# One pass per sorted block of tokens instead of two masked experts: the mixture stage of a one-core transformer kernel

## The chip, the cores and the metric

The kernel runs on 1 core of one Trainium2 chip. The metric is the device time of one execution in microseconds (us). Besides the engines (TensorE for matrix products, VectorE, ScalarE, GpSimd and SyncE, which issues the plain transfers) the core has 16 transfer (DMA) engines. In the profile they are named PE (with PEld for its weight loads), DVE, ACT, POOL and SP.

## The reference, cut to what matters

The input is 4096 tokens (2 x 2048) of 256 floats. Six residual stages follow each other: a mixture stage, a linear attention, the same mixture stage again (same weights), an FP4 feed-forward, a softmax attention, and the FP4 feed-forward again. The change touches the two mixture stages only. Each computes

```
gate_scores = xf @ gate_w.T                       # two experts
one_hot = one_hot(argmax(softmax(gate_scores)))
masked = xf[None] * one_hot.T[:, :, None]         # zero rows for the expert not chosen
h = relu(einsum('end,edh->enh', masked, w1) + b1[:, None, :])
expert_out = einsum('enh,ehd->end', h, w2) + b2[:, None, :]
routing_output = expert_out.sum(axis=0)
shared = relu(xf @ sw1 + sb1) @ sw2 + sb2
x = x + 0.5 * (routing_output + shared)           # xf is the layer-normalised x
```

with 256 features and 1024 hidden units. The expert that is not chosen sees a zero row and so still adds the constant `relu(b1) @ w2 + b2`.

## The kernel before

Everything is written as one program of raw blocks; within a block each engine's instructions stand in the order written, and semaphores order the engines against each other. `x` stays in on-chip memory as 32 tiles of 128 tokens. Products are made at nearly full precision: each operand is split into a rounded part (`hi`) and a remainder (`lo`), and three matmuls (hi x hi, hi x lo, lo x hi) are summed.

The mixture stage, `ffn0(tag)`, is called twice, with tag "a" and tag "b". It works through G = 8 groups of 4 tiles (512 tokens). A group has 24 steps: 8 hidden chunks of 128 units for each of the shared expert and the two routed ones. A step s has these parts:

- TensorE, `up(g, s)` (lines 365 to 376): 6 matmuls of 512 columns into one PSUM bank of three.
- ScalarE, `hidden` (lines 433 to 449): two activations, the rounded and the full relu. For the routed steps VectorE first multiplies by the mask (`masking`, line 525), which zeroes the hidden sums of tokens that belong to the other expert.
- VectorE, `low` (line 531): the remainder, full minus rounded.
- TensorE, `down(g, s - 2)` (lines 378 to 393): 12 matmuls of 256 columns, which add to the group's output banks.

Once in a group TensorE also makes the gate's product (line 409, 6 matmuls of 512 columns), and VectorE two masks of it (lines 516 and 517). The normalised tokens of the next group are made by VectorE (`normal`), transposed by TensorE after steps 18 and 21 (line 349), copied by ScalarE (`evacuate`, line 425) and completed by VectorE (`low_x`, line 503) in steps 19 and 22. The next group's first `up` waits for that, two steps later. `finish` (line 540) adds the group's output to x and makes the statistics for the next stage's layer norm (`tile_stats`, lines 119 and 121).

Weights come in pieces of 128x512 through two buffers (line 333). At the start eight pieces of the shared expert are split, by GpSimd (lines 605 and 607) and by ScalarE and VectorE in turn (lines 453 and 509); then come three bias rows, which in call "a" stand in SP's queue behind seven loads of x (line 336), and VectorE sums them (lines 570 and 574) before its first `low`; then GpSimd splits the 16 pieces of the two routed experts.

Of the kernel before, what the change touches and what calls it, by code (L numbers as in the profile page):

```python
# [9 lines left out]
I32 = mybir.dt.int32  # L10
ALU = mybir.AluOpType
# [3 lines left out]
P = 128  # L15
# [41 lines left out]
def build_program(nc, A):  # L57
# [21 lines left out]
    with ExitStack() as ctx:  # L79
# [153 lines left out]

        def ffn0(tag):
            with ExitStack() as scope:
                w1 = [sb(f"w1{p}_{tag}", [P, NE, KD, H0], F32R, scope) for p in ("hi", "lo")]
                w2 = [sb(f"w2{p}_{tag}", [P, NE, C0, D], F32R, scope) for p in ("hi", "lo")]
                b1 = sb(f"b1_{tag}", [P, NE * C0], scope=scope)
                b2h = sb(f"b2h_{tag}", [P, D], scope=scope)
                gate_w = [sb(f"gate_{p}_{tag}", [P, KD, P], F32R, scope) for p in ("hi", "lo")]  # L240
                gcol = sb(f"gate_cols_{tag}", [P, KD, NE - 1], scope=scope)
                gdiff = sb(f"gate_diff_{tag}", [P, KD], scope=scope)
                XN = ring(scope, f"xn{tag}", [P, D], 2)
                XT = ring_of_pairs(scope, f"xT{tag}", [P, KD, GW], 2)
                mask = sb(f"mask{tag}", [P, NE - 1, GW], scope=scope)
                HB = ring(scope, f"hid{tag}", [P, GW], 2)
                HS = ring_of_pairs(scope, f"hs{tag}", [P, GW], 3)
                RAW = ring(scope, f"raw{tag}", [P, GW], 2)

                raw_in = [event(f"f0_raw_in{i}", 16) for i in range(2)]  # L250
                turned, gcol_ok, gate_ok, b1_ok, b2_ok = (event(f"f0_{n}") for n in ("turned", "gcol", "gate", "b1", "b2"))
                split_hi, split_pool, split_vec = (event(f"f0_split_{n}") for n in ("hi", "pool", "vec"))
                xn_ok, xturn, xhi, xlo = (event(f"f0_{n}") for n in ("xn", "xturn", "xhi", "xlo"))
                stat_in, std_g, prod, gmask = (event(f"f0_{n}") for n in ("stat_in", "std", "prod", "gmask"))
                masked, hid_ok, low_ok, down_ok = (event(f"f0_{n}") for n in ("masked", "hid", "low", "down"))
                biased, done = event("f0_biased"), event("f0_done")

                NP = 2 * C0 // 2
                STEPS = NE * C0
                PPG = STEPS + 1  # L260

                def place(g, s):

                    return g * PPG + s + (1 if s >= 4 else 0)

                def read_of(n):

                    g, i = divmod(n, PPG)
                    if i == 4:
                        return gmask(g + 1)  # L270
                    s = i - (1 if i > 4 else 0)
                    if s < C0:
                        return hid_ok(g * STEPS + s + 1)
                    return masked(g * 2 * C0 + s - C0 + 1)
# [4 lines left out]

                def item_of(ex, p):  # L280
                    return 2 + p if ex == 0 else 13 + (ex - 1) * NP + p

# [7 lines left out]
                def piece_dst(ex, p):  # L290
                    if p < 4:
                        return [w[:, ex, p % 2, p // 2 * GW:(p // 2 + 1) * GW] for w in w1]
                    return [w[:, ex, 2 * (p - 4):2 * (p - 4) + 2, :].rearrange("p c d -> p (c d)") for w in w2]

                def piece_ok(ex, p):

                    if ex == 0:
                        return split_vec(p // 2 + 1) if p % 2 else split_pool(p // 2 + 1)
                    return split_pool(4 + (ex - 1) * NP + p + 1)

                def raw_free(item):
                    if item < 2:
                        return turned(item + 1)
                    if item < 10:
                        return piece_ok(0, item - 2)
                    if item < 13:
                        return b2_ok(item - 9)
                    return piece_ok(1 + (item - 13) // NP, (item - 13) % NP)

                with nc.Block() as block:  # L310

                    @block.sync
                    def _(e):
                        e.dma_start(RAW[0][0:2, 0:D], A["L0_ffn_gate_w"]).then_inc(*raw_in[0].up)
# [25 lines left out]
                    def _(e):  # L340
                        def transposes(g, i):
# [3 lines left out]
                            if n:  # L345
                                e.wait_ge(*xlo(n))
# [1575 lines left out]
```

## Time and profile before

| | us |
|---|---|
| three timed runs | 3766.29, 3769.75, 3779.08; median 3769.75 |
| the profiled execution | 3781.05 |
| its span, first to last instruction | 3779.3 |
| first mixture stage, first product to last | about 19.2 to 606 |
| second mixture stage, first product to last | about 968.5 to 1547.5 |

All durations below come from the one profiled execution. Busy TensorE time is modelled, since its matmuls overlap: the distance between the starts of two neighbouring matmuls says how fast they follow each other, while the duration of one is longer. Start times are us from the span's start.

### The profile page before, as it was taken

What the parts mean: (1) busy time and instruction counts of PE and PEld (TensorE: products, weight loads), DVE (VectorE), ACT (ScalarE), POOL (GpSimd) and SP (SyncE); (2) the same over time, 40 slices, a digit from 0 to 9 for tenths busy, and PEclk for the clock granted to TensorE, in tenths of its full rate; (3) what the DMA queues carried; (4) which work ended last, traced back from release to release, by engine and by line L of the source; (5) the groups of instructions that cost most, each with busy time, mean ns of one, the idle gap of its engine ahead of it and who ended that gap; (6) DMA issues with size and microseconds to landing.
All of it is one profiled execution on the core that took longest, in us unless ns stands there. A gap on an engine that the chain in (4) does not pass through costs nothing. (4 is left out here: it accounts for less than half of the span.)

```text
span 3779.3 us, 57424 instructions
## 1 busy us (share of the span) xinstructions
PE 3535.4 (94%) x22274; PEld 2399.2 (63%) x22274; DVE 2698.2 (71%) x4907; ACT 2136.2 (57%) x3830; POOL 600.5 (16%) x504
## 2 busy tenths in 40 slices
PE   6999998999799999799789999999999999999799
PEld 6888886777688888799534433333333333333798
DVE  4545544786454454799478888889889999882898
ACT  3444443443344444455327777777777777766555
POOL 4000001444400000355200000000000000000565
PEclk9999999999899999899969999899999999888899
DMA  3000001000200000000240211111021120000000
GB/s 116 1 1 1 1 1 40 2 2 1 72 1 1 1 1 1 1 1 1 64 50 13 46 24 21 16 20 17 9 28 14 22 28 8 2 2 1 6 18 23
DMA packets 34455, 63.93 MB, mean 17 GB/s; under 512 B 4309, under 2 KB 23433, under 8 KB 31113
## 3 DMA queue, kind: packets, MB, share of 16 engines
q1 hardware_dynamic: 34184, 60.27, 8.5%
q8 instruction: 177, 2.90, 0.3%
q14 instruction: 94, 0.76, 0.1%
HBM read 47.02 MB, written 13.11 MB: 16 GB/s over the span
## 5 line engine op out<-in xcount | busy, mean ns | idle before, releaser
L1836 DVE TENSOR_REDUCE smxp<-psum 128x1 f32<-128x512 f32 x2048 | 1276.3, 682 | 175.3 <-PE psum L1701 168.8
L1796 ACT ACTIVATE spr<-psum 128x512 f32<-128x512 f32 x2048 | 1082.3, 599 | 470.9 <-PE psum L1720 462.2
L1720 PE MATMUL psum<-sqs,sks 50*128 50x512 f32 x2048 | 754.6, 470 | 6.4 <-ACT spr L1796 3.1
L1701 PE MATMUL psum<-sks,sqs 48*128 48x512 f32 x2048 | 677.1, 457 | 29.5 <-DMA sqs<-q_parts 29.1
L1701 PEld LDWEIGHTS psum<-sks,sqs 48*128 48x128 f32 x2048 | 292.3, 198 | 538.7 <-issue 461.3
L1734 PE MATMUL psum<-spr,sv 128*32 128x512 f32 x4096 | 576.8, 636 | 1.8 <-ACT spr L1796 0.7
L1720 PEld LDWEIGHTS psum<-sqs,sks 50*128 50x128 f32 x2048 | 323.1, 194 | 200.9 <-ACT spr L1796 170.0
L1455 POOL MEMSET fhqb<- 128x64 f32 x3 | 0.3, 152 | 1668.9 <-POOLq L1616 1668.9
L389 PE MATMUL psum<-w2hi_a,hsa_hi 128*128 128x256 f32 x768 | 217.2, 283 | 16.8 <-DVE hsa_lo L531 16.8
L389 PE MATMUL psum<-w2hi_b,hsb_hi 128*128 128x256 f32 x768 | 217.3, 283 | 9.2 <-DVE hsb_lo L531 9.2
L389 PE MATMUL psum<-w2lo_b,hsb_hi 128*128 128x256 f32 x768 | 217.8, 284 | 0.0
L389 PE MATMUL psum<-w2lo_a,hsa_hi 128*128 128x256 f32 x768 | 217.7, 283 | 0.0
L389 PE MATMUL psum<-w2hi_a,hsa_lo 128*128 128x256 f32 x768 | 217.3, 283 | 0.0
L389 PE MATMUL psum<-w2hi_b,hsb_lo 128*128 128x256 f32 x768 | 217.3, 283 | 0.0
L525 DVE TENSOR_TENSOR hidb<-psum,maskb 128x512 f32<-128x512 f32 x128 | 88.3, 690 | 173.3 <-PE psum L355 173.3
L531 DVE TENSOR_TENSOR hsb_lo<-hidb,hsb_hi 128x512 fp32r<-128x512 f32 x192 | 147.3, 768 | 84.1 <-ACT hidb L444 75.8
L531 DVE TENSOR_TENSOR hsa_lo<-hida,hsa_hi 128x512 fp32r<-128x512 f32 x192 | 146.4, 763 | 83.8 <-ACT hida L444 75.4
L525 DVE TENSOR_TENSOR hida<-psum,maska 128x512 f32<-128x512 f32 x128 | 88.1, 688 | 158.9 <-PE psum L355 158.9
L447 ACT ACTIVATE hsb_hi<-hidb,b_b 128x512 fp32r<-128x512 f32 x128 | 92.6, 724 | 183.7 <-DVE hidb L525 183.7
L447 ACT ACTIVATE hsa_hi<-hida,b_a 128x512 fp32r<-128x512 f32 x128 | 92.7, 724 | 173.5 <-DVE hida L525 173.5
L1734 PEld LDWEIGHTS psum<-spr,sv 128*32 128x32 f32 x4096 | 82.9, 110 | 152.9 <-issue 126.5
L389 PEld LDWEIGHTS psum<-w2hi_a,hsa_hi 128*128 128x128 f32 x768 | 146.1, 190 | 28.2 <-DVE hsa_lo L531 20.5
(345 smaller groups left out, 7183.3 us busy)
## 6 DMA issues: line engine op xcount, KB each, us to landing
sks<-q_parts SPq DMA_DIRECT2D x48, 256.0 KB, 8.9
sqs<-q_parts SPq DMA_DIRECT2D x48, 256.0 KB, 20.0
q_parts<-spart SPq DMA_DIRECT2D x16, 512.0 KB, 2.7
x<-in_L_attn_x_dram SPq DMA_DIRECT2D x8, 512.0 KB, 7.3
rawa<-in_L_ffn_w_dram SPq DMA_DIRECT2D x16, 256.0 KB
rawb<-in_L_ffn_w_dram SPq DMA_DIRECT2D x16, 256.0 KB
out_dram<-x SPq DMA_DIRECT2D x8, 512.0 KB, 2.9
rawa<-in_L_ffn_sw_dram SPq DMA_DIRECT2D x8, 256.0 KB
```

What stands on the lines that cost most here:

```text
L389: m = e.matmul(ops[:, i // 2, (i % 2) * D:(i % 2 + 1) * D], hs[u][:, i * P:(i + 1) * P], w2[v][:, ex, c, :], start=(s == 0 and i % 2 == 0 ...
L447: e.activation(hi[:], hid[:], ACT.Relu, bias=bias).then_inc(*sc.up())
L525: e.tensor_tensor(HB[n % 2][:], psum[:, j % 3, :], mask[:, s // C0 - 1, :], ALU.mult).then_inc(*masked.up)
L531: e.tensor_tensor(lo[:], HB[n % 2][:], hi[:].bitcast(F32), ALU.subtract).then_inc(*low_ok.up)
L1455: m = e.memset(hq[:, H1:], 0.0)
L1701: e.matmul(bank(what), QS[n % 2][rows, pr, q0:q0 + P], KS[n % 2][rows, pr, jc * GW:(jc + 1) * GW], start=True, stop=True, tile_position=(H ...
L1720: e.matmul(st[s % 3], KS[n % 2][rows, pr, jt * P:(jt + 1) * P], QS[n % 2][rows, pr, ic * GW:(ic + 1) * GW], start=True, stop=True, tile_po ...
L1734: m = e.matmul(po[32 * hq:32 * hq + VW, :], VB[b][:, jt, c0:c0 + VW], PR[j % 2][:, hq, :], start=(jt == 0), stop=(jt == TB - 1), tile_posi ...
L1796: e.activation(PR[j % 2][:, hq, :], st[s % 3], ACT.Exp, scale=float(DH) ** -0.5).then_inc(*exp_ok.up)
L1836: e.tensor_reduce(out[:, r // (2 * GT * IC), r // (2 * IC) % GT, r // 2 % IC, r % 2:r % 2 + 1], bank(what), AX.X, ALU.max).then_inc(*pm_fr ...
```

## The change

A mixture stage no longer runs both routed experts over every token. VectorE computes the gate of each token as a sum over x (a `scalar_tensor_tensor` with an accumulated output, 32 of them). TensorE counts with two small triangular and all-ones products how many tokens of each expert stand ahead of a token, and from that each token gets a row in a table in DRAM: the first expert's from the front, the second's from the back. GpSimd scatters all 32 normalised tiles there by indirect DMA. The 4096 sorted rows are then 8 blocks of 512, of which at most one is mixed.

The stage now has 17 passes of 8 steps: 4 shared passes (groups 0 to 3), 9 routed passes, and 4 shared passes (groups 4 to 7). The routed passes are the 8 blocks, each with the expert that a register names, and the mixed block once more with the second expert. For `up`, GpSimd copies 128x512 weights of the named expert to a fixed buffer for each step; `down` reads its moving operand at an address from a register. The output rows go to a second table in DRAM, from which GpSimd gathers them back, 128 rows to a DMA, and VectorE adds them to x two tiles to a step during the last passes (`add_back`). The constant of the expert not chosen is computed once, with 48 matmuls of 256 columns in the fourth shared pass (`constant_rows`). The masks, the masking and the gate's product go.

Passes are 8 steps long, so the transposes of the next pass's tokens stand after steps 4 and 6 of each pass (6 and 7 in the fourth), where they stood after 18 and 21 of 24. ScalarE's order shows what this does to the hand-over between two groups. Before, at the end of a group (`xTa_hi` is the copy of the transposed tokens, `hsa_hi` and `hida` the two activations of a step):

```order
L425 ACTIVATE xTa_hi<-psum 128x2x256
L447 ACTIVATE hsa_hi<-hida,b_a 128x512
L449 ACTIVATE hida<-hida,b_a 128x512
L443 ACTIVATE hsa_hi<-psum,b_a 128x512
L444 ACTIVATE hida<-psum,b_a 128x512
```

A whole step (24th, L447 and L449) stands between the copy and the next group's first step (L443 and L444). Now, at the end of a routed pass, ScalarE has:

```order
L568 ACTIVATE hsa_hi<-psum,bwa 128x512
L569 ACTIVATE hida<-psum,bwa 128x512
L544 ACTIVATE xTa_hi<-psum 128x2x256
L568 ACTIVATE hsa_hi<-psum,bwa 128x512
L569 ACTIVATE hida<-psum,bwa 128x512
```

The copy stands directly ahead of the next pass's first step, and behind the two activations of the last step.

VectorE's order at the last passes, where the gathered rows (`yoa`) are added to x; `hsa_lo` is `low`, once in a step:

```order
L727 TENSOR_TENSOR hsa_lo<-hida,hsa_hi 128x512
L783 SCALAR_TENSOR_TENSOR x<-yoa,x 128x256
L120 BN_STATS stats<-x 128x6
L122 BN_AGGR mv<-stats 128x2
L783 SCALAR_TENSOR_TENSOR x<-yoa,x 128x256
L120 BN_STATS stats<-x 128x6
L122 BN_AGGR mv<-stats 128x2
L716 TENSOR_TENSOR xTa_lo<-psum,xTa_hi 128x2x256
```

Each step now has six instructions beside `low`, where `finish` had them once in 24 steps.

GpSimd's order from the splits of the first pieces on; `f_sorted_a` is the table in DRAM:

```order
L878 DMA f_sorted_a<-xga,pos_i_a 4096x256 x8
L871 TENSOR_TENSOR w_a<-yoa,w_a 128x512 x8
L878 DMA f_sorted_a<-xga,pos_i_a 4096x256 x4
L884 DMA f_sorted_a<-yoa,pos_i_a 4096x256 x16
L878 DMA f_sorted_a<-xga,pos_i_a 4096x256 x4
L933 TENSOR_LOAD expert_a
```

Before, GpSimd issued no DMA at all. The 16 rows of line 884 are the tiles of groups 4 to 7, staged by ScalarE through four buffers.

The core of the diff:

```diff
+SF = 4
+NR = G + 1
+PASSES = G + NR
+END = PASSES * C0
+BIG = 2 if tag == "a" else 1
+AHEAD = 1 if tag == "a" else 4
+AB = [(1 + k // 4 % 2, 4 + k % 4 if k < 8 else k % 4) for k in range(16)]
+AB_STEP = [(10 if tag == "a" else 4) + k if k < 8 else (18 if tag == "a" else 13) + k - 8 for k in range(16)]
+STAGE_STEP = 17 if tag == "a" else 10
...
+ADD_STEP = (SF + NR + 1) * C0 + 5
...
+def turn_steps(p):
+    return (C0 - 2, C0 - 1) if p == SF - 1 else (4, 6)
...
+        def rows_in(r):
+            p = SF + r
+            e.wait_ge(*xturn(2 * (p - 2) + 2))
+            e.dma_start(XG[p % 2][:], sorted_x[r * GW:(r + 1) * GW, :].rearrange(
+                "(t p) d -> p t d", p=P)).then_inc(*xs_in[p % 2].up)
+        def rows_out(r):
+            e.wait_ge(*done(2 * (SF + r + 1)))
+            e.dma_start(routed_y[r * GW:(r + 1) * GW, :].rearrange("(t p) d -> p t d", p=P),
+                        YO[r % 2][:]).then_inc(*y_out[r % 2].up)
...
+            if r is not None and r < G:
+                e.wait_ge(*copied(r * C0 + c + 1))
+                w = [WR[n % 2][:, v] for v in range(2)]
+            else:
+                w = [w1[:, v, 0 if r is None else NE - 1, :, c * P:(c + 1) * P] for v in range(2)]
...
+            ex = 0 if r is None else NE - 1 if r == G else 1 + chosen[r]
...
-                                 hs[u][:, i * P:(i + 1) * P], w2[v][:, ex, c, :],
...
+                                 hs[u][:, i * P:(i + 1) * P], w2[:, v, ex, c, :],
...
+        def constant_rows(q):
+            if q == 0:
+                e.wait_ge(*pos_ok(SF))
+                e.wait_ge(*split_pool(12))
+            e.wait_ge(*lo_rows(q + 1))
+            rb = (rb_hi, rb_lo)
+            for c in range(4):
+                for j, (u, v) in enumerate(((0, 0), (0, 1), (1, 0))):
+                    m = e.matmul(psum[:, 3, q // 2 * D:(q // 2 + 1) * D], rb[u][:, c, :],
+                                 w2[:, v, 1 + q // 2, q % 2 * 4 + c, :], start=(q == c == j == 0),
+                                 stop=(q % 2 == 1 and c == 3 and j == 2), skip_group_check=True)
+            m.then_inc(*rows_used.up)
...
-        for g in range(G):
-            for s in range(STEPS):
-                if s == 4:
-                    ps = buffer(g * PPG + 4)
-                    product(ps, gate_w, XT[g % 2])
-                up(g, s)
-                if s >= 2:
-                    down(g, s - 2)
-                if g + 1 < G and s in (18, 21):
-                    transposes(g + 1, (s - 18) // 3)
...
+        for n in range(END):
+            p, c = divmod(n, C0)
+            if n == SF * C0:
...
+                chosen = nc.values_load_multi_w_load_instructions(
...
+            up(n)
+            if n >= 2:
+                down(n - 2, chosen)
+            if p < SF and c == 1:
+                ranks(p)
+            if p == SF - 1 and 2 <= c < 6:
+                constant_rows(c - 2)
+            if p + 1 < PASSES and c in turn_steps(p):
+                transposes(p + 1, turn_steps(p).index(c))
+        down(END - 2, chosen)
+        down(END - 1, chosen)
...
+        def stage(k):
+            t = SF * GT + k
+            if k == 0:
+                e.wait_ge(*nmr_ok(G - SF if tag == "a" else 1))
+            if k >= GT:
+                e.wait_ge(*stage_out[k % GT](k // GT))
+            e.activation(YO[1][:, k % GT, :], x[:, t, :], ACT.Identity, bias=nmr[:, t:t + 1],
+                         scale=rstd[:, t:t + 1]).then_inc(*staged.up)
...
+        def high_rows(q):
+            if q == 0:
...
+                e.wait_ge(*rows_used(q))
+            e.activation(rb_hi, b1r[:, 4 * q:4 * q + 4].unsqueeze(2).to_broadcast([P, 4, P]),
+                         ACT.Copy).then_inc(*hi_rows.up)
...
+            if p + 1 < PASSES:
+                if p == SF - 1 and c in turn_steps(p):
+                    evacuate(p + 1, turn_steps(p).index(c))
+                if p != SF - 1 and c - 1 in turn_steps(p):
+                    evacuate(p + 1, turn_steps(p).index(c - 1))
...
+        def gates(t, n):
+            for j in range(t, t + n):
+                if tag == "a":
+                    if j % GT == 0:
+                        e.wait_ge(*x_in_ok[j // GT](1))
+                    tile_stats(e, j, stat_in)
+                    e.wait_ge(*stat_in(j + 1))
+                small(e.scalar_tensor_tensor(out=junk, in0=x[:, j, :], scalar=mv[:, j, 0:1], in1=gdiff,
+                                             op0=ALU.subtract, op1=ALU.mult, accum_out=gate[:, j:j + 1]))
...
-        def masking(g, s):
-            n, j = g * STEPS + s, place(g, s)
-            e.wait_ge(*prod(j + 1))
-            e.wait_ge(*low_ok(n - 1))
-            e.tensor_tensor(HB[n % 2][:], psum[:, j % 3, :], mask[:, s // C0 - 1, :],
-                            ALU.mult).then_inc(*masked.up)
...
+        def low_rows(q):
+            e.wait_ge(*hi_rows(q + 1))
+            if q:
+                e.wait_ge(*rows_used(q))
+            e.tensor_tensor(rb_lo, b1r[:, 4 * q:4 * q + 4].unsqueeze(2).to_broadcast([P, 4, P]),
+                            rb_hi.bitcast(F32), ALU.subtract).then_inc(*lo_rows.up)
...
+        def add_back(k):
+            t = BACK[k]
+            e.wait_ge(*back_in[k % (2 * GT)](k // (2 * GT) + 1))
+            if t // GT < G - 1:
+                e.wait_ge(*done(2 * (t // GT if t // GT < SF else t // GT + NR) + 2))
+            e.scalar_tensor_tensor(out=x[:, t, :], in0=YO[k // GT % 2][:, k % GT, :], scalar=0.5,
+                                   in1=x[:, t, :], op0=ALU.mult, op1=ALU.add).then_inc(*added.up)
+            e.wait_ge(*added(k + 1))
+            if t // GT < G - 1:
                 tile_stats(e, t)
...
+        def scatter(k):
+            e.wait_ge(*pos_ok(k + 1))
+            for j in range(GT):
+                t = k * GT + j
+                e.indirect_dma_start(sorted_x, bass.IndirectOffsetOnAxis(pos_i[:, t:t + 1], 0),
+                                     XG[k % 2][:, j, :], None).then_inc(*group_out[k % 2].up)
+            if k == BIG:
+                for i in range(REST):
+                    t = SF * GT + i
+                    e.wait_ge(*staged(i + 1))
+                    e.indirect_dma_start(sorted_x, bass.IndirectOffsetOnAxis(pos_i[:, t:t + 1], 0),
+                                         YO[1][:, i % GT, :], None).then_inc(*stage_out[i % GT].up)
+        def copies(r, chosen):
+            p = SF + r
+            if r >= 2:
+                e.wait_ge(*hid_ok((p - 1) * C0))
+            e.tensor_copy(BW[r % 2][:], b1[:, 1 + chosen[r], :]).then_inc(*bias_ok.up)
+            for c in range(C0):
+                n = p * C0 + c
+                if r or c >= 2:
+                    e.wait_ge(*prod(n - 1))
+                e.tensor_copy(WR[n % 2], w1[:, :, 1 + chosen[r], :, c * P:(c + 1) * P]).then_inc(*copied.up)
+                if r == G - 2 and c % 2:
+                    mixed(c // 2)
+        def mixed(j):
+            if j == 0:
+                e.wait_ge(*xturn(2 * (SF + G - 2) + 2))
+            e.indirect_dma_start(XG[(SF + G) % 2][:, j, :], None, sorted_x,
+                                 bass.IndirectOffsetOnAxis(mixed_i[:, j:j + 1], 0)).then_inc(
+                *mixed_in.up)
...
+        for k, t in enumerate(BACK):
+            if k >= 2 * GT:
+                e.wait_ge(*added(k - 2 * GT + 1))
+            e.indirect_dma_start(YO[k // GT % 2][:, k % GT, :], None, routed_y,
+                                 bass.IndirectOffsetOnAxis(back_i[:, t:t + 1], 0)).then_inc(
+                *back_in[k % (2 * GT)].up)
```

## Rows read from the trace of the kernel before

**Rows 1.** The page: busy us of each engine, share of the span, instructions.
```profile
PE 3535.4 (94%) x22274; PEld 2399.2 (63%) x22274; DVE 2698.2 (71%) x4907; ACT 2136.2 (57%) x3830; POOL 600.5 (16%) x504
```

**Rows 2.** Busy time in four stretches of the two mixture stages, granted clock, DMA.
```profile
19.20:39.00 19.80, 6.45 (x18) 4.79 (x18) 3.53 (x7) 3.01 (x5) 2.42 (x3) 0.78 0.78 245
39.00:606.00 567.00, 563.50 (x3542) 506.55 (x3542) 288.88 (x510) 272.67 (x401) 52.80 (x40) 1.00 0.03 8
968.40:980.40 12.00, 6.28 (x18) 4.65 (x18) 3.13 (x8) 3.18 (x6) 2.38 (x3) 0.78 0.38 98
980.40:1547.50 567.10, 563.54 (x3541) 506.61 (x3542) 275.36 (x448) 270.57 (x394) 51.78 (x40) 0.99 0.03 8
```

**Rows 3.** Timeline, one step: start, duration, engine, line, operation, idle before.
```profile
598.34 0.28 PE L389 MATMUL psum<-w2hi_a,hsa_hi 128*128 128x256 f32 x1
...
599.77 0.39 PE L355 MATMUL psum<-xTa_hi,w1hi_a 128*128 128x512 f32 x1
...
601.17 0.28 PE L389 MATMUL psum<-w2hi_a,hsa_hi 128*128 128x256 f32 x1
```

**Rows 4.** Timeline, a transposition between two products.
```profile
303.37 0.60 PE L349 MATMUL psum<-ident,xna 128*128 128x128 f32 x4
...
303.73 0.48 PE L355 MATMUL psum<-xTa_hi,w1hi_a 128*128 128x512 f32 x1
```

**Rows 5.** Timeline, the heads of calls "a" and "b".
```profile
23.22 1.08 DVE L509 TENSOR_TENSOR w2lo_a<-rawa,w2hi_a 128x512 fp32r<-128x512 f32 x1 [3.32 <-ACT w2hi_a L453]
...
39.04 0.58 PE L389 MATMUL psum<-w2hi_a,hsa_hi 128*128 128x256 f32 x1 [13.37 <-DVE hsa_lo L531]
...
973.32 0.69 DVE L509 TENSOR_TENSOR w2lo_b<-rawb,w2hi_b 128x512 fp32r<-128x512 f32 x1 [3.96 <-ACT w2hi_b L453]
...
980.49 0.58 PE L389 MATMUL psum<-w2hi_b,hsb_hi 128*128 128x256 f32 x1 [5.72 <-DVE hsb_lo L531]
```

**Rows 6.** Groups of 39:606: busy us, mean ns of one, idle before.
```profile
L443 ACT ACTIVATE hsa_hi<-psum,b_a 128x512 fp32r<-128x512 f32 x62 | 42.7, 688 | 119.4 <-PE psum L355 75.9 <-issue 28.0 <-DVE hsa_lo L531 13.5
L444 ACT ACTIVATE hida<-psum,b_a 128x512 f32<-128x512 f32 x62 | 42.2, 681 | 0.0
...
L503 DVE TENSOR_TENSOR xTa_lo<-psum,xTa_hi 128x512 fp32r<-128x512 f32 x14 | 9.7, 691 | 20.9 <-ACT xTa_hi L425 20.9
L540 DVE SCALAR_TENSOR_TENSOR x<-psum,x 128x512 f32<-128x512 f32 x14 | 9.4, 670 | 0.0
...
L425 ACT ACTIVATE xTa_hi<-psum 128x512 fp32r<-128x512 f32 x14 | 8.1, 577 | 0.0
```

**Rows 7.** Timeline, statistics of two tiles in call "a".
```profile
5.14 0.40 DVE L119 BATCH_NORM_STATS2 stats<-x 128x6 f32<-128x256 f32 x1
...
5.67 0.39 DVE L119 BATCH_NORM_STATS2 stats<-x 128x6 f32<-128x256 f32 x1
```

**Rows 8.** Single lines, ns min/median/max: three operations on 128x256.
```profile
L574 DVE SCALAR_TENSOR_TENSOR b2h_a<-rawa,b2h_a x2: 424/425/426, 35.1 to 38.0; 128x256 f32<-128x256 f32 x2
...
L124 DVE TENSOR_SCALAR xna<-x,mv,rstd x32: 404/408/417, 10.7 to 524.1; 128x256 f32<-128x256 f32 x32
...
L1338 ACT ACTIVATE fxna<-x,foffa,rstd x32: 584/601/604, 1553.4 to 1787.2; 128x256 f32<-128x256 f32 x32
```

**Rows 9.** The same view: GpSimd's splits; and its longest single operation (timeline).
```profile
L605 POOL CAST w1hi_a<-rawa x10: 603/610/1067, 7.7 to 68.1; 128x512 fp32r<-128x512 f32 x10
...
L607 POOL TENSOR_TENSOR w1lo_a<-rawa,w1hi_a x10: 1264/1298/1626, 8.4 to 68.8; 128x512 fp32r<-128x512 f32 x10
...
1553.60 3.23 POOL L1452 TENSOR_TENSOR fwg_loa<-wgT,fwg_hia 128x1408 fp32r<-128x1408 f32 x1 [1.46 <-ACT fwg_hia L1353]
```

**Rows 10.** DMA issues: KB each, median us from issue to landing.
```profile
q_parts<-spart SPq DMA_DIRECT2D x16, 512.0 KB, 2.7
```

**Rows 11.** Timeline: three `low` of VectorE beside one GpSimd operation.
```profile
979.75 4.49 DVE L531 TENSOR_TENSOR hsb_lo<-hidb,hsb_hi 128x512 fp32r<-128x512 f32 x3
979.91 2.76 POOL L613 TENSOR_TENSOR x<-x,b2h_b 128x1024 f32<-128x1024 f32 x1 [6.74 <-DVE b2h_b L574]
```

More of the change, by code:

```diff
@@ new lines, in ffn0 @@
+                gdiff, junk = other[:, 0, :], other[:, 1, :]
+                WR = [rows[:].rearrange("p (s k n) -> p s k n", s=2, k=KD) for rows in ROWS]
+                before = sb(f"before_{tag}", [P, P], BF16, scope)
+                ones = sb(f"ones_{tag}", [P, P], BF16, scope)
+                table_i = sb(f"table_i_{tag}", [P, T + G + GT], I32, scope)
+                table = sb(f"table_{tag}", [P, T + G + GT], scope=scope)
+                place_of, limit, row_of = table[:, 0:T], table[:, T:T + G], table[:, T + G:T + G + GT]
@@ new lines, in ffn0 @@
+                gate = sb(f"gate_{tag}", [P, T], scope=scope)
+                first = sb(f"first_{tag}", [P, T], BF16, scope)
+                second = sb(f"second_{tag}", [P, T], scope=scope)
+                sums = sb(f"sums_{tag}", [P, T], scope=scope)
+                ahead = sb(f"ahead_{tag}", [P, T], BF16, scope)
+                total = sb(f"total_{tag}", [P, 2], BF16, scope)
+                shift = sb(f"shift_{tag}", [P, T], scope=scope)
+                pos = sb(f"pos_{tag}", [P, T], scope=scope)
@@ new lines, in ffn0 @@
+                batch_ok, ranked, pos_ok, route_ok = (event(f"f0_{n}") for n in ("batch", "ranked", "pos", "route"))
+                staged, hi_rows, lo_rows, rows_used, other_ok = (event(f"f0_{n}") for n in ("staged", "hi_rows", "lo_rows", "rows_used", "other"))
+                prod, hid_ok, low_ok, down_ok, done = (event(f"f0_{n}") for n in ("prod", "hid", "low", "down", "done"))
+                bias_ok, copied, added = (event(f"f0_{n}") for n in ("bias", "copied", "added"))
+                group_out = [event(f"f0_group_out{i}", 16) for i in range(2)]
@@ L551, in _ @@
                             rstd_of(e, 0, T)
[L552 to L560 removed]
+                            shifts(SF * GT, REST)
@@ new lines, in _ @@
+                        scattered(e)
+                        e.wait_ge(*split_vec(12))
+                        e.wait_ge(*rows_used(4))
+                        e.wait_ge(*route_ok(1))
+                        chosen = nc.values_load_multi_w_load_instructions(
+                            expert[0:1, :], engines=[mybir.EngineType.Pool], min_val=0, max_val=NE - 2,
+                            skip_runtime_bounds_check_because="each is the outcome of a comparison, 0 or 1")[1]
+                        for r in range(G):
+                            copies(r, chosen)
```

632 lines of the change are left out of this document (398 added, 234 removed).

## The prediction

> **What bounds the kernel now.** I read the page first: PE is busy 94% of the span [rows 1], the other engines far less. That share mixes six stages, so the two mixture stages were read by stretches [rows 2]. From the first `down` to the end of a call TensorE is busy 563.5 of 567.0 us at a granted clock of 1.00, with VectorE and ScalarE at about half. So a step costs what its matmuls cost, and removing matmuls removes time until another engine or a hand-over is late. The timeline gives the price: from the first `down` matmul of a step to that of the next is 601.17 - 598.34 = 2.83 us, of which twelve matmuls of 256 columns take 1.43 (0.119 each) and six of 512 take 1.40 (0.233 each) [rows 3]. I use 2.84 for a step. A set of four transposes costs 303.73 - 303.37 = 0.36, and about 0.08 at the next weight load, so 0.45 [rows 4].
>
> **The sum of TensorE's work, per call.** Before: 24 steps in 8 groups = 192; after: 8 steps in 17 passes = 136. The number of passes is written in the code and does not depend on the tokens.
> - 56 steps less: 56 x 2.84 = -159.0.
> - The gate's product, 8 x 6 x 0.233 = -11.2.
> - Transposes: 32 sets behind the first `down` instead of 14: 18 x 0.45 = +8.1.
> - `constant_rows`: 48 x 0.119 = +5.7. The ranking products have at most 16 columns and are left at nothing beside it.
>
> Together -156.4, against 567.0 before. The masking on VectorE goes too, but it was hidden: VectorE was busy 289 of the 567 us [rows 2].
>
> **The hand-over between passes, once per pass.** This is the largest cost I find. The second set of transposes stands in step 6 of 8, and ScalarE copies it behind the two activations of step 7. From the end of `up` in step 7 to the next pass's first `up`: two activations 0.69 + 0.68, the copy 0.58, `low_x` 0.69 [rows 6], some 0.2 for four hops, so 2.84. Meanwhile TensorE has one `down` of 1.43. It waits 1.4. Before, a whole step more stood between, and it waited for nothing. 16 hand-overs: +22.4 per call. If a hop is free or costs double, 1.2 to 1.6.
>
> **The constant rows.** In the fourth pass four products each wait for a ScalarE copy (about 0.6) and a VectorE remainder (0.69) that can only follow that step's two activations: 1.4 of waiting again, four times: +5.6. VectorE also has the routing's ten small operations there; bounds 3 to 10.
>
> **VectorE as the bound.** In call "a" it makes statistics and gates of two tiles a step for 14 steps. A tile's statistics recur every 0.53 us [rows 7]; the gate is one more pass over 128x256 with a wait, like the 0.43 of [rows 8] and about 0.1. Two tiles 2.1, `low` 0.69, `finish` (2 x 0.67), `low_x` (2 x 0.69) and `normal` (4 x 0.41 [rows 8]) over 8 steps 0.54, reciprocals about 0.3: 3.65 against TensorE's 2.84. 14 x 0.81 = 11.3, less one hand-over that falls into it: +10 in "a". In "b" the statistics exist, and 2.5 stays below 2.84. In `add_back` two tiles cost 2 x (0.43 + 0.53 + 0.06) = 2.04, with `low` and the same 0.54 that is 3.27: 16 x 0.43 = 6.9, less two hand-overs: +4 per call.
>
> **Staging.** ScalarE stages two tiles a step (0.60 each [rows 8], 1.2) beside 1.37 of activations and 0.63 of a weight split: 3.2, so 8 x 0.36 = 2.9. It also waits for a buffer until an earlier scatter has landed, and the first scatter stands behind eight GpSimd splits (1.3 each [rows 9]) that ScalarE's own order feeds; that leaves the first round some 3 us late. +6 per call; bounds 0 and 25, the upper from the second rival below.
>
> **What the trace of before does not show.**
> - GpSimd's DMA: 32 scatters, 4 and 32 gathers per call. An issue is bounded below by a 128x512 cast, 0.61, above by its longest operation, 3.23 [rows 9]; I take 1.3, the `tensor_tensor` over 128x512, which also touches every partition. A store of 512 KB to DRAM landed in 2.7 [rows 10]; one scatter has 128 KB, so I take no more. At 1.3 two issues fit a step (threshold 2.84 / 2 = 1.42), and the block loads behind the last scatter have some 10 us of cover. Cost 0.
> - GpSimd's weight copies in 64 steps: 0.61 to 1.3 [rows 9], each with over 4 us between the release of its buffer and its use. Cost 0. They can hold VectorE back: three `low`, worth 2.05, took 4.49 beside one GpSimd operation [rows 11]. A copy delays a `low` by at most its own 1.3, and `low` has about 3.5 us to spare, so 0 also.
> - Reading eight registers, on TensorE once per call, while its array drains: between 0 and 3, I take +1.
> - 768 `down` matmuls per call with an address from a register. The address is computed twice in a step, and TensorE's sequencer runs ahead, so I take 0 more than 0.119. The upper bound is that none overlaps with its predecessor: 0.28 each [rows 3].
>
> On the registers, the Trainium skill (DMA: Bandwidth & Descriptors, Latency and other measured facts) gives a `tensor_load` a floor of about 600 ns. No run here shows one yet; by it my 1 us stands as it is.
>
> **The clock.** TensorE is granted 1.00 in the busy stretches, and 0.78 in the two heads, where it idles [rows 2]. 20 short waits per call may cost some of it. One head lost 0.22 x 19.8 = 4.4 us by it; three such losses per call are the upper bound, 13, none the lower, and I take +3.
>
> **The heads.** In "a" the three bias rows no longer stand ahead of the first `low`. Before, the last split of the head ended at 24.3 and `down` began at 39.04 [rows 5]. Now the table cast and first batch (1.3), two gates (2.2) and `low` (0.7) follow, plus 0.5 for the later first load: 29.1. -9.9. In "b" the split ended at 974.0 and `down` began at 980.49 [rows 5]; now 16 gates at 0.49 come first: 974.0 + 0.5 + 1.3 + 7.8 + 1.0 + 0.7 = 985.3: +4.9.
>
> **The sum.** Waits per call: 22.4 + 5.6 + 4 + 6 + 1 + 3 = 42. Call "a": -156.4 + 42 + 10 - 9.9 = -114.3. Call "b": -156.4 + 42 + 4.9 = -109.5. Together -223.8. The profiled execution took 3781.05, 11.3 above the median of the timed runs, so 3557.3 as profiled and 3546 as timed. The other four stages are untouched.
>
> **Rivals.**
> 1. *Only TensorE's work counts.* The hand-overs and constant rows are hidden after all (28 per call): 3546 - 56 = 3490. For it: TensorE idled only 3.5 of 567.0 us before [rows 2], though VectorE and ScalarE stand between its products all the time. Against it: the order of ScalarE, which puts the copy last.
> 2. *GpSimd's DMA is slow.* Above 1.42 us per issue the 16 staged scatters and 24 of the gathers set the pace. At 3 us, near the upper bound: 40 x 1.58 = 63 per call, 3546 + 126 = 3672. For it: nothing in this trace has such DMAs, and VectorE, with which GpSimd collides [rows 11], is busiest there. The Trainium skill (SBUF — State Buffer, its box on how DVE blocks DMA) says that GpSimd cannot write descriptors while VectorE runs in a two-port mode, 3100 ns instead of 620; its figure would give 3.1 for mine of 3. Here that mode would have to hold in most of VectorE's operations, and `low` and `add_back` have two inputs each.
> 3. *Addresses from registers are a little dear*, 0.04 each: 1536 x 0.04 = 61, 3607.
> 4. *Slower than before*: each such matmul waits for its predecessor, at 0.283 instead of 0.119. 1536 x 0.164 = +252, 3798. It turns the result from 223.8 / 1536 = 0.146 us apiece. For it: no such operand in the trace. Against it: the address does not change within a step.
>
> **Chances.** Forecast 3546 with its own range of 3505 to 3590: 0.60. Rival 1: 0.17. Rival 2: 0.14. Rival 3: 0.06. Rival 4: 0.03. The range 3485 to 3640 takes in the forecast and rivals 1 and 3. About 0.3% (11 us) is what a measurement can tell from no change. Faster 0.95: all but rival 4 and some of the worst mixtures of 2 and 3; same 0.01; slower 0.04.
>
> **What will show it.** A `down` pitch of 0.119 in the routed passes (rival 3 or 4 otherwise). A gap of 1.2 to 1.6 ahead of each pass's first `up`, ended by VectorE's `low_x` (rival 1: none). ScalarE waiting for DMA at the staged tiles, VectorE at `add_back` only if rival 2 holds. Each call from first `down` to end: about 463 in "a" and 453 in "b". The forecast is wrong if either is off by over 20.

## The result, and the profile after

| | before | after |
|---|---|---|
| median of the timed runs, same chip | 3774.41 (3766.29 to 3809.56) | 3525.39 (3518.08 to 3544.6) |
| ratio | | 0.933, 95% interval 0.926 to 0.940 |
| the profiled execution | 3781.05 | 3527.95 |

The change is faster by about 249 us. The forecast was 3546; the interval of the ratio, times the 3769.75 known then, gives 3491 to 3544, and the median was 3525.39. So the forecast was some 20 us too slow.

First the page of the kernel after, then stretches of it, one to a line: pass 1 of call "a" (passes are numbered from 0; in these lines each runs from its first `down` to the next pass's), the eight routed passes that follow pass 3, the whole call "a" from its first `down` to its end, the head of "b" (from its first `up` to its first `down`), call "b" from its first `down`, and all that follows. They answer to [rows 1] and [rows 2]. Columns: span of the stretch, busy time and instructions of each engine, granted clock, DMA share, GB/s.

```profile
span 3526.1 us, 54173 instructions
...
PE 3206.8 (91%) x20420; PEld 2115.6 (60%) x20420; DVE 2558.7 (73%) x4892; ACT 1999.8 (57%) x3714; POOL 735.0 (21%) x740
```

```profile
64.40:99.80 35.40, 28.94 (x160) 25.47 (x159) 27.92 (x75) 16.63 (x30) 14.01 (x12) 0.86 0.21 68
175.80:372.80 197.00, 186.59 (x1213) 168.89 (x1212) 63.41 (x96) 88.34 (x144) 41.36 (x70) 1.00 0.11 36
...
30.61:492.39 461.78, 414.64 (x2615) 371.87 (x2615) 219.29 (x489) 205.14 (x343) 117.93 (x148) 0.97 0.16 53
856.77:875.09 18.32, 8.24 (x21) 5.98 (x22) 13.75 (x50) 3.22 (x7) 2.77 (x3) 0.59 0.17 57
875.09:1317.40 442.31, 405.93 (x2616) 366.39 (x2614) 192.92 (x398) 203.48 (x336) 118.67 (x148) 0.98 0.16 50
1317.40:3526.00 2208.60, 2055.54 (x12192) 1112.17 (x12192) 1869.04 (x3329) 1437.46 (x2718) 329.91 (x273) 0.95 0.12 19
```

Call "a" from its first `down` fell from 567.1 to 461.8, call "b" from 567.3 to 442.3. Eight routed passes take 197.0, so 24.6 each. 23.2 of that are 8 steps and two sets of transposes; the rest is one wait. Pass 1, the first line, is dearer: 35.4, at a granted clock of 0.86.

Where TensorE waited in call "a": engine and line, what ended the wait, us in total, times, the longest.

```profile
PE psum L458 <- DVE xTa_lo L716: 17.5, 8, 4.5
PE psum L458 <- issue: 10.6, 8, 1.5
PE psum L438 <- DVE xTa_lo L716: 7.9, 3, 6.0
PE psum L504 <- DVE rowsa L734: 5.1, 4, 1.3
PE psum L438 <- DVE xga L125: 4.4, 2, 3.0
```

Line 458 is `up`: its 16 waits are the hand-overs. Line 504 is the constant rows. Line 438 is the transposes, which wait in the first passes only. The distances between the starts of matmuls give the same waits some 0.1 to 0.2 larger: together, with some smaller ones that the lines above leave out, 52.2 in "a" and 39.7 in "b".

One hand-over, with the last `down` ahead of it and, above, a `down` in a routed pass. Columns: start, duration, engine, line, tiles, in brackets the idle time before.

```profile
210.67 0.40 PE L475 MATMUL psum<-w_a,hsa_hi 128*128 x2
...
211.96 0.28 PE L475 MATMUL psum<-w_a,hsa_lo 128*128 x1
212.08 0.60 PE L438 MATMUL psum<-ident,xga 128*128 128x128 f32 x4
...
214.14 0.69 ACT L568 ACTIVATE hsa_hi<-psum,bwa 128x512 fp32r<-128x512 f32 x1 [1.95 <-issue]
...
214.73 0.68 ACT L569 ACTIVATE hida<-psum,bwa 128x512 f32<-128x512 f32 x1
...
215.18 0.28 PE L475 MATMUL psum<-w_a,hsa_lo 128*128 x1
215.30 0.60 ACT L544 ACTIVATE xTa_hi<-psum 128x512 fp32r<-128x512 f32 x1
215.92 0.69 DVE L716 TENSOR_TENSOR xTa_lo<-psum,xTa_hi 128x512 fp32r<-128x512 f32 x1 [3.01 <-ACT xTa_hi L544]
...
216.72 0.47 PE L458 MATMUL psum<-xTa_hi,rowsa 128*128 128x512 f32 x1 [1.26 <-issue]
```

Twelve `down` matmuls with an address from a register take 212.08 - 210.67 = 1.41, or 0.117 each: no more than in [rows 3]. Then the chain is as forecast: two activations, the copy (line 544), the remainder (line 716), and the next `up` 1.54 after the last `down` began, 0.12 of which is that matmul's own. So TensorE waited 1.42.

GpSimd's DMA, by start and duration, in the staging of call "a":

```profile
104.79 0.98 POOL L878 DMA_INDIRECT f_sorted_a<-xga,pos_i_a  x1 [0.30 <-issue]
106.07 0.96 POOL L884 DMA_INDIRECT f_sorted_a<-yoa,pos_i_a  x1 [0.30 <-issue]
107.33 0.96 POOL L884 DMA_INDIRECT f_sorted_a<-yoa,pos_i_a  x1 [0.30 <-issue]
```

Neighbours begin 1.26 to 1.28 apart; I had taken 1.3. The longest scatter of line 884 in either call took 1.33, the longest gather 1.14. So the slow issues of the second rival did not occur. That says nothing against the page that I had named for it: the Trainium skill (SBUF — State Buffer, its box on how DVE blocks DMA and the section behind it) has a GpSimd DMA wait for its descriptors beside a VectorE in a two-port mode, 3.1 us instead of 0.62. No row here tells in which mode a VectorE operation ran. What the trace shows is that the operations of this kernel did not bring it about, though they kept VectorE busy for 30.9 of the 42.7 us from 449.70 to 492.39, where the last gathers are.

### The profile page after: what moved, and what is told of

Its sections match the earlier page's. It is cut to its first block and busy times, and to the rows that moved or that the text cites. A ratio compares the mean times of both kernels' runs of the same rounds, so it can differ in the third digit from the quotient of the medians.

```text
span 3526.1 us, 54173 instructions
## 1 busy us (share of the span) xinstructions
PE 3206.8 (91%) x20420; PEld 2115.6 (60%) x20420; DVE 2558.7 (73%) x4892; ACT 1999.8 (57%) x3714; POOL 735.0 (21%) x740
## 5 line engine op out<-in xcount | busy, mean ns | idle before, releaser
L475 PE MATMUL psum<-w_a,hsa_hi 128*128 128x256 f32 (+1 forms) x1088 | 201.7, 284 | 2.3 <-DVE hsa_lo L727 1.7
L727 DVE TENSOR_TENSOR hsb_lo<-hidb,hsb_hi 128x512 fp32r<-128x512 f32 x136 | 95.5, 702 | 147.2 <-ACT hidb L569 141.6
L727 DVE TENSOR_TENSOR hsa_lo<-hida,hsa_hi 128x512 fp32r<-128x512 f32 x136 | 93.6, 688 | 147.9 <-ACT hida L569 137.9
L475 PE MATMUL psum<-w_b,hsb_hi 128*128 128x256 f32 (+1 forms) x1088 | 199.7, 282 | 0.0
L475 PEld LDWEIGHTS psum<-w_a,hsa_hi 128*128 128x128 f32 x1088 | 179.5, 192 | 15.8 <-DVE hsa_lo L727 3.0
L475 PEld LDWEIGHTS psum<-w_b,hsb_hi 128*128 128x128 f32 x1088 | 177.9, 191 | 11.8
L475 PE MATMUL psum<-w_a,hsa_lo 128*128 128x256 f32 (+1 forms) x544 | 153.4, 282 | 0.7 <-issue 0.7
L475 PE MATMUL psum<-w_b,hsb_lo 128*128 128x256 f32 (+1 forms) x544 | 153.0, 281 | 0.0
L458 PE MATMUL psum<-xTa_hi,w_a 128*128 128x512 f32 x288 | 110.9, 427 | 18.9 <-DVE xTa_lo L716 17.5
L458 PE MATMUL psum<-xTb_hi,w_b 128*128 128x512 f32 x288 | 108.4, 418 | 15.2 <-DVE xTb_lo L716 13.8
```

The costliest lines, as they stand in the source:

```text
L458: m = e.matmul(psum[:, n % 3, :], w[u][:, k, :], XT[p % 2][v][:, k, :], start=(k == j == 0), stop=(k == KD - 1 and j == 2))
L475: m = e.matmul(ops[:, i // 2, (i % 2) * D:(i % 2 + 1) * D], hs[u][:, i * P:(i + 1) * P], w2[:, v, ex, c, :], start=(c == 0 and i % 2 == 0 ...
L727: e.tensor_tensor(lo[:], HB[n % 2][:], hi[:].bitcast(F32), ALU.subtract).then_inc(*low_ok.up)
```

## The experiments

**The two kernels once more.** No edit.

> The changed kernel once more, as the base for the runs beside it, and for the stages that the change does not touch. Its first trace is 253 us shorter than the trace before, of which 22.9 us lie behind the second mixture stage (2231.7 to 2208.8), where no instruction changed. Theory A: that part is the granted clock, which differs from run to run (0.93 and 0.95 there): this run's stretch lies between 2200 and 2240 and goes with its clock. Rival: the change itself shortens it, and it is again within 5 us of 2208.8.

> The kernel before once more, for its trace. Theory A (the stretch behind the second mixture stage varies with the granted clock): 2200 to 2240 us, shorter when its clock is above 0.93. Rival (the first trace is what this kernel always does): within 5 us of 2231.7.

Measured: 3519.8 against 3781.89 for before, ratio 0.9329 (0.9253 to 0.9405). The lengths of the calls repeat to about 1%: "a" from its first `down` 456.2, "b" 439.0, before 566.7 and 567.5. Of the 5.6 us that "a" is shorter, 3.3 are in pass 2 (34.3 instead of 37.6) and 2.5 are in two passes of `add_back` (24.8 and 24.8 instead of 25.7 and 26.4). A difference of a few us in "a" between two kernels is therefore no more than one kernel shows by itself. The part behind the second mixture stage, which no edit touches, took 2200.9 here and 2208.7 in the first profile of the changed kernel; the two profiles of the kernel before had 2231.5 and 2235.2.

**Fixed address in `down` (third and fourth rivals).** Every `down` of the routed passes uses the last expert's weights, so that the outputs are another function.

```diff
-ex = 0 if r is None else NE - 1 if r == G else 1 + chosen[r]
+ex = 0 if r is None else NE - 1
```

> The second products of the routed passes take the first layer's partner of the second expert at a fixed address instead of the one that the register names (GpSimd's copies still go by the register). Theory (an address from a register costs TensorE nothing): a routed pass still takes 24.65 us. Rival (it costs 0.04 us for each of 96 matmuls of a pass, or the two register operations stop the sequencer): 1 to 4 us less per pass, 9 to 36 us per call.

Measured: routed passes of 24.7, as with registers; "a" 461.3 (after: 461.8 and 456.2), "b" 440.3 (442.3 and 439.0). The one time taken, 3553.6, is 25.7 longer than the profiled execution of after, but its untouched part behind the second mixture stage took 2237.7, which is 29.0 longer. A `down` of a routed pass and what follows it, to be held beside the 1.41 above:

```profile
210.49 0.40 PE L475 MATMUL psum<-w_a,hsa_hi 128*128 128x256 f32 x2
...
211.90 0.60 PE L438 MATMUL psum<-ident,xga 128*128 128x128 f32 x4
```

1.41 too. The address from a register costs nothing that can be seen: both rivals fall.

**Without the constant rows.**

```diff
-if p == SF - 1 and 2 <= c < 6:
-    constant_rows(c - 2)
```

(and the same for `high_rows` and `low_rows`; `others` no longer adds the products, and two waits that `constant_rows` held stand elsewhere, so the outputs are another function)

> Leaves out the constant of the expert that is not chosen: its 48 matmuls per call, the copies and remainders that feed them, and their addition. Theory (each of the four products waits 1.4 us and works 1.4 us): 4 x 2.8 = 11.3 us per call, 22.6 us faster than the changed kernel. Rival (these steps are cover for the scatter and the block load that follow it, so without them TensorE waits for the first block instead): a wait of several us before the first routed pass, and less than 12 us faster.

Measured: "a" 441.4 (14.8 less than the profile of the same job), "b" 427.5 (11.5 less): 13 per call, where I had 5.7 for the matmuls and 5.6 for the waits, 11.3. "b" fits; the 3.5 more in "a" are within what "a" moves by itself. The rival of the expectation falls: the first routed pass starts behind the same wait of 1.64. Whole: 3512.6, ratio 0.928 (0.921 to 0.936), 7 us less than the kernel after in the same job where 22.6 were expected. That alone would tell little, since the part behind took 2230 here, 29 longer than in the profile of `after_again`.

**The transposes one step earlier.** `x1_turn35` turns after steps 3 and 5, `normal` one step earlier too. `x12_turn35` is the same kernel, timed another time.

```diff
-return (C0 - 2, C0 - 1) if p == SF - 1 else (4, 6)
+return (C0 - 2, C0 - 1) if p == SF - 1 else (3, 5)
-if g is not None and c in (3, 5):
+if g is not None and c in (2, 4):
```

> The transposes of the next pass stand after steps 3 and 5 instead of 4 and 6, and the normalising one step earlier; the fourth pass keeps its places. Theory (the hand-over is what TensorE waits for, 1.42 us at each of the 16 boundaries of a call): the gap of 1.42 vanishes at the boundaries of the routed passes, a routed pass takes 23.2 us instead of 24.65, and the kernel is about 40 us faster than the changed one (15 boundaries, 2 calls, 1.4 us; up to 8 of them kept back where VectorE is late). Rival (VectorE and ScalarE are late by themselves and the wait moves to another place in the pass): the gap appears at a later step and the kernel is under 10 us faster.

> The turns alone once more, beside x10_const2 on the same chip. The ratio to the kernel before should be 0.923 again (0.919 to 0.927). If the softmax attention's time moves with the run and not with the kernel, the tail behind the second mixture stage is anywhere in 2200 to 2238 in the three profiles, whichever of them has which edit.

Measured: 3481.9, ratio 0.923 (0.916 to 0.930), 38 less than the kernel after in the same job; the other time 3474.8, 0.918 (0.913 to 0.923). In `x12_turn35`, the end of a routed pass, to be held beside the hand-over above:

```profile
219.63 0.60 ACT L544 ACTIVATE xTa_hi<-psum 128x512 fp32r<-128x512 f32 x1
220.26 0.69 DVE L716 TENSOR_TENSOR xTa_lo<-psum,xTa_hi 128x512 fp32r<-128x512 f32 x1 [3.01 <-ACT xTa_hi L544]
...
222.06 0.40 PE L475 MATMUL psum<-w_a,hsa_hi 128*128 x2
222.30 0.28 PE L475 MATMUL psum<-w_a,hsa_lo 128*128 x1
222.41 0.39 PE L458 MATMUL psum<-xTa_hi,rowsa 128*128 128x512 f32 x1
```

The remainder is done at 220.95, and `up` follows its predecessor at 0.11. A routed pass takes 23.2. TensorE's waits in "b" of this kernel, in place of the five kinds of above:

```profile
PE psum L438 <- DVE xTb_lo L716: 7.1, 1, 7.1
PE psum L504 <- DVE rowsb L734: 5.1, 4, 1.3
PE psum L458 <- issue: 1.5, 1, 1.5
```

16 hand-overs at 1.4 and dearer were there. 15 of them are gone; the one that is left, 1.5, leads from the fourth pass to the first routed one, whose transposes the edit did not move. In `x1_turn35` "a" is 28.3 and "b" 25.2 shorter than in `after_again`.

**Staging three steps later.**

```diff
-STAGE_STEP = 17 if tag == "a" else 10
+STAGE_STEP = 20 if tag == "a" else 13
```

> ScalarE stages the 16 tiles of groups 4 to 7 three steps later (steps 20 to 27 instead of 17 to 24 in a, 13 to 20 instead of 10 to 17 in b). Theory (ScalarE, in order, waits for the first scatter to land and holds up the copy of the transposed tokens: the waits of 6.2 us in a and 7.4 us in b ahead of the third or second pass's last transposes): these waits fall to under 2.5, 4 to 8 us less per call. Rival (the wait comes from VectorE or from GpSimd's rate of 1.26 us per DMA, whenever it starts): it moves three steps and keeps its size, and later scatters delay the first routed block.

Measured: 3514.9 once. ScalarE no longer waits for a buffer at line 582 (after: 4.4 in "a", 8.1 in "b"). The pass where it had waited shrank, from 37.6 to 29.0 in "a" and from 35.6 to 27.7 in "b", but the next ones grew: 38.4 to 41.4 in "a", 25.0 to 31.2 and 36.9 to 39.5 in "b". Net 1 to 7 less in "a" and 1.4 less to 1.9 more in "b". So the wait mostly moved, and the one buffer did not set the time. Which of the other engines does is not shown by this run; the next speaks for VectorE in "a".

**A gate over 16 of the 256 features.** Another routing follows from it, of the same size.

```diff
-e.scalar_tensor_tensor(out=junk, in0=x[:, j, :], ...
+e.scalar_tensor_tensor(out=junk[:, 0:16], in0=x[:, j, 0:16], ...
```

> The gate of a token is summed over its first 16 features only, so tokens go to other experts; all else is the changed kernel. It takes about 0.25 us of VectorE from each of 64 tiles. Theory (in call a VectorE sets the pace of the first 14 steps; in call b only the 16 gates ahead of the first step cost): the body of a is 28 x 0.25 = 5 to 7 us shorter than 456 to 462, the head of b 3 to 4 us shorter than 18.4, the body of b within 2 us of 439 to 442. Rival (TensorE waits in the first passes of a for staging and for the hand-overs, not for the gates): the body of a is within 2 us of before.

Measured once: head of "b" 14.2 instead of 18.3; passes 0 to 3 of "a" (here from first `up` to first `up`) 31.2, 33.3, 35.3, 37.0 instead of 33.8, 35.4, 37.6, 38.4. These four together are 8.5 shorter than in the first profile of after and 5.4 shorter than in the second; the whole "a" is 8.4 and 2.8 shorter. From the first `down` of "a" to that of its first routed pass VectorE was busy for 79.4 instead of 88.1, so 8.7 less, and the time is 9.3 or 6.0 less. So about as much as VectorE was spared, the passes became shorter: VectorE's work sets most of their pace, as far as one profile against two that differ by 3.3 can show it. The body of "b" is unchanged.

**All edits at once, with the gates of "b" spread.** Four gates ahead and four a step, not 16 ahead and two a step; the turns of above; and the constant rows' copy ahead of its step's activations, its remainder right behind `low`.

```diff
-hidden(n)
+if p == SF - 1 and 2 <= c < 6:
+    high_rows(c - 2)
+hidden(n)
...
-    gates(0, AHEAD * GT)
+    gates(0, GT)
```

> Three edits together: transposes after steps 3 and 5; the copies and remainders for the constant rows ahead of the step's two activations and right behind low, where they stood behind them; in b only 4 gates ahead of the first step, then 4 in each step. Theory: -38 as measured for the first alone; the four waits of 1.4 us per call ahead of the constant products vanish (-11); the head of b falls from 18.4 to about 12.5 and its first passes lose 2 to 3 (-3): about 52 us less than the changed kernel, span 3460 to 3475 at the clock of its first trace. Rival (the order within ScalarE and VectorE pushes low or the hand-over late instead): gaps of over 1 us reappear in the fourth pass, and less than 44 in all.

Measured: 3484.4 once. To be held beside it is `x10_const2` below, which has the same edits but for the gates. The head of "b" fell from 18.4 there to 12.4, but "b" itself took 423.0 instead of 408.1: the transposes wait for VectorE for 15.2 us in 5 places, against 7.3 in 2. Six gained, fifteen lost, where the expectation had three. The whole is 35 to 41 less than the changed kernel, where 52 were expected. This edit is dropped.

**The turns and the constant rows; and with staging later in "a".**

> Turns after steps 3 and 5 (as x1_turn35), and in the fourth pass ScalarE's copy of a constant row ahead of the step's two activations, VectorE's remainder right behind the preceding low. The gates of call b stay as in the changed kernel (16 in the head, then 2 a step). If the four waits of 1.4 us are only the place of copy and remainder in their engines' order, they go here as in x7_all and nothing comes in their place: some 5 per call less than x1_turn35, so 3472 and a ratio of 0.920 to 0.923. Rival: the copy moved ahead delays the activations by 0.6 and TensorE waits for those instead; then the same as x1_turn35, 3482.

> x10_const2 and, in call a alone, the staging of tiles three steps later (as x4_stage3 did it in both calls). If x4_stage3's small gain in a (1 to 7) adds up: 1 to 6 below x10_const2. Rival: with passes of 23.2 us the staging has less time until the first block load, and the later passes lose what the earlier ones gain: 0 to 5 above it.

Measured, in one job with `x12_turn35` (before: 3777.74):

| | median | ratio, 95% | "a" | "b" | behind |
|---|---|---|---|---|---|
| x12_turn35 | 3474.8 | 0.918 (0.913 to 0.923) | 426.6 | 413.8 | 2215.6 |
| x10_const2 | 3465.9 | 0.918 (0.913 to 0.923) | 420.1 | 408.1 | 2222.1 |
| x11_const2_stage | 3460.8 | 0.915 (0.909 to 0.921) | 417.8 | 408.3 | 2204.6 |

Moving the constant rows made "a" 6.4 and "b" 5.7 shorter: their waits are gone, and all that took their place is one of 0.6 in "a". In x10 the waits in "b" are

```profile
PE psum L438 <- DVE xTb_lo L715: 7.3, 2, 7.1
PE psum L458 <- issue: 1.5, 1, 1.5
```

The whole times can't tell the three apart. The stages show 12 us for the constant rows; the 2 of the later staging are less than "a" moves by itself and are not shown to be a gain. All three are faster than the changed kernel and about 8% faster than the one before. The intervals of their ratios, up to 0.923, lie below those of the change, from 0.925 up, though the two were not timed together; the difference of the ratios is 55 to 68 us, that of the lengths of "a" and "b" against `after_again` 55 to 69.

## Why the prediction was right, and where it was off

Profile against profile the time fell by 253.1, where the sum said 223.8. The mechanism was right: TensorE's removed work, less a wait at each hand-over. By stretches (each from the end of the one before):

| | predicted | measured |
|---|---|---|
| start to the end of "a" | -114.3 | -113.7 |
| between the mixture stages | 0 | +2.0 |
| "b", from its first `up` | -109.5 | -118.7 |
| behind "b" | 0 | -22.8 |

- *TensorE's work.* Right in kind, but too little removed, by 10 to 12: take the waits out of x12_turn35 (26.0 and 14.7) and 400.6 and 399.1 are left, where 567.0 - 156.4 gives 410.6. Two things were missed. A step of after takes 2.80 (twelve `down` at 0.117), where I had 2.84 for all 136. And the 567.0 were not all work: 192 steps of 2.83, less two `up` ahead of the first `down`, with gate and transposes, are 558. The other 9 are in the trace of before. Its first step took 5.19 (39.04 to 44.23), 2.4 more than the others, at a granted clock of 0.52, which is about the lower of the two levels (1.2 GHz), after TensorE had idled for 13.37 us [rows 5]. And at each of the 7 changes of group TensorE waited 0.65 in a `down`, and with three shorter pauses behind it lost about 1 us:

```profile
39.04:44.30 5.26, 5.26 (x19) 4.73 (x20) 3.75 (x2) 1.26 (x2) 5.18 (x4) 0.52 0.16 50
...
104.50 0.27 PE L389 MATMUL psum<-w2hi_a,hsa_lo 128*128 128x256 f32 x1
105.27 0.39 PE L389 MATMUL psum<-w2hi_a,hsa_hi 128*128 128x256 f32 x1 [0.49 <-DVE hsa_lo L531]
```

  VectorE made `low_x` and the masking ahead of that `low`. The 3.5 us of idling in the prediction are these seven, 0.49 each by the view. So "it waited for nothing" is wrong: the old order had a wait at each hand-over too, a shorter one. I carried these 7 us over and then added all the new ones.
- *Hand-overs, 1.4 each.* Right: 1.42 in nearly all routed passes. The 16 together are 30.6 in "a" and 26.7 in "b" (22.4 predicted), because those in the first passes are dearer (up to 4.6), as is one at `add_back` (2.4 and 3.3, but 1.47 in `after_again`). Moving the turns by one step took away 14 of 16 in "a" and 15 in "b", as the reason given for them says. So the first rival, that they were hidden, falls.
- *Constant rows, 5.6 of waits.* Measured 1.49, 1.40, 1.40, 1.40: 5.7. The matmuls were +5.7 by the sum; leaving both out gave 11.5 and 14.8.
- *VectorE and staging in the first passes.* In "a" the sum had 10 + 6. What was measured beyond the regular hand-over in passes 0 to 3: 15.3 of waits at transposes and `down`, and 6 of dearer hand-overs, 21. In "b" 6 were predicted and 7.4 + 1.2 came. That VectorE is behind most of it in "a" fits the run with the shorter gate.
- *`add_back`, +4.* Right in the first profile only. Its passes took 25.7, 26.4 and 25.3 in "a" and 26.7, 26.4 and 25.3 in "b" instead of 24.7: 3.3 and 4.3, part of it waits and part the clock (0.97 in that stretch of "a"). In `after_again` they took 24.8, 24.8 and 25.3 in both calls, 0.8 more than 24.7 each, at a clock of 1.00. So +4 is not a cost of each execution; what made it in the first is not shown.
- *GpSimd.* Right: 1.26 between issues, weight copies of 0.61. No wait of TensorE has its origin there in the routed passes.
- *Reading the registers, +1.* Nothing is seen of it. The load on TensorE's queue took 0.78 in "a" and 0.61 in "b":

```profile
L522 PEldq TENSOR_LOAD <-expert_a x1: 781/781/781, 163.9 to 163.9; - x1
...
165.06 0.60 PE L438 MATMUL psum<-ident,xga 128*128 128x128 f32 x4
...
165.69 0.60 ACT L544 ACTIVATE xTa_hi<-psum 128x512 fp32r<-128x512 f32 x1 [0.53 <-PE psum L438]
...
167.11 0.47 PE L458 MATMUL psum<-xTa_hi,rowsa 128*128 128x512 f32 x1 [1.46 <-issue]
```

  The load was done at 164.7, and TensorE's matmuls went on until the transposes ended at 165.66; only then came the wait ahead of the first routed pass. That wait is 1.64 by the starts and not 1.42, but here ScalarE's copy waited for the transposes, which stand behind the last step in the fourth pass. The Trainium skill's floor of about 600 ns for a `tensor_load` (DMA: Bandwidth & Descriptors, Latency and other measured facts) agrees with 0.78 and 0.61 and with 0.79 and 0.59 on GpSimd's queue.
- *The clock, +3 per call.* Off in "a". Without waits, "a" took 461.8 - 52.2 = 409.6 and "b" 402.6, against 400.6 and 399.1 with the turns moved. So about 9.0 and 3.5. Passes 1 and 2 of "a" ran at 0.86, each with waits; the routed ones at 1.00.
- *The lengths from these.* "a" was to be 462.6: -10.0 for the work, +3.2 for waits (52.2 against 49), +6.0 for the clock, 461.8. That it came out within 1 us is luck: the errors cancel. "b" was to be 452.6: -11.5, +0.7 and +0.5, 442.3.
- *Heads.* `down` of "a" at 30.6 (29.1 predicted), head of "b" 6.3 longer than before (4.9 predicted).

The largest miss has no term in the sum. It took "The other four stages are untouched" to mean that they cost the same. No instruction of them changed, and the part behind "b" still took 22.8 less. In the ten further profiles of changed kernels it took 2200.9 to 2237.7. Two rows of it, in kernels that are alike there (the second begins 3 us late and ends 1 early; in full this part took 2230.0):

```profile
1547.50:3779.00 2231.50, 2079.24 (x12195) 1121.64 (x12194) 1869.45 (x3329) 1439.05 (x2718) 329.19 (x273) 0.93 0.12 18
```

```profile
1290.00:3516.00 2226.00, 2076.81 (x12192) 1116.77 (x12192) 1869.10 (x3322) 1438.71 (x2718) 327.34 (x273) 0.94 0.12 18
```

The first is the kernel before, the second x2_noconst, so a changed one, which here takes as long as before. VectorE and ScalarE are busy to 0.1% the same as in the kernel after; only TensorE, at 0.93 and 0.94 and not at 0.95, was busy 21 to 24 us longer. Over all 13 profiles the length of this part and TensorE's busy time in it go together: 2200.9 with 2048.6 at one end, 2237.7 with 2084.8 at the other. Changed kernels stand at both ends. So the 22.8 go with the granted clock of one execution. Why that clock differs is not shown.

Whether the mean of this part differs stays open. An estimate: the two profiles of before have 1548 and 1555 us ahead of it; their mean, taken off 22 timed executions, leaves 2227 on average, from 2200 up. 33 timed executions of the changed kernel and its variants, less what each one's profile has ahead, leave 2218. That takes the stages ahead as constant, which they are only to some us. By this some 10 of the 22.8 may be the change's after all, by a way that no run shows; the rest is the luck of one execution. Without the 22.8 the profiled gain is 230.3, against 223.8.

## What to carry to other kernels

Count the removed matmuls by the distance of their starts, and the gain of the edited stages comes out within a few per cent (here 223.8 against 230.3, with errors that partly cancel). Then walk each hand-over once in the order of the engines, in the old kernel too: one copy that stands behind the last step's activations cost 1.4 us sixteen times per call, and one step earlier it cost nothing. When a wait is taken away in a stretch where three engines are loaded (the staging), look at the next passes before you count it as won. Judge an edit worth under 1% by the length of its own stage, since here a part that no edit touches moved by 37 us over the profiles. Even the edited stage moves: "a" by 5.6 us in two profiles of one kernel.

## What the runs showed of the hardware

- The part behind "b" (softmax attention between two FP4 feed-forwards), at a granted clock of 0.93 to 0.95, moved by 1.7% (2200.9 to 2237.7) over the profiles, while VectorE's busy time in it stayed at 1869 to 1873 us.
- An indirect DMA of 128 rows took 0.94 to 1.00 us of GpSimd in 118 of 136 cases in the kernel after, and it was 0.30 until the next; the longest was 1.46. VectorE was busy for 30.9 of 42.7 us beside some of them.
- Twelve matmuls whose moving operand has an address from a register took 1.41 us (212.08 - 210.67), as twelve with a fixed one (211.90 - 210.49 in the kernel with the fixed address).
- Loading eight registers on TensorE's queue took 0.78 and 0.61 us while its matmuls went on.
- After 13.37 us of idling TensorE made its first step at a granted clock of 0.52 and in 5.19 us; the steps after it took 2.83 at 1.00 (kernel before, call "a").
